# A conditioned residual stack on one core: both grouped convolutions moved to sixteen 32x32 tiles of TensorE, on unrounded fp32

## What is computed

```
# L0, L3: groups = 4 (32 channels in, 32 out each), 9 taps, padding 4
out = conv(x, weight, groups=4) + (c @ c_weight.T)[:, :, None] + bias[None, :, None]
# L1, L2: 8 experts, att = softmax(mlp(c)), one set of shares per sample
agg_w = einsum('bk,koi->boi', att, weight)
out   = einsum('boi,bih->boh', agg_w, x) + (att @ bias_k)[:, :, None]
# the chain
x = x + L0(x); x = x + L1(x); x = x + L2(x); x = x + L3(x)
```

## Time and profile before

| | |
|---|---|
| median of 3 executions | 2600.23 us |
| profiled execution | 2600.42 us |
| its span in the trace | 2598.5 us |
| TensorE busy | 2554.9 us, 98% of the span, 11082 matmul records |
| TensorE weight loads busy | 2071.6 us, 80% |
| VectorE busy | 2277.4 us, 88% |
| ScalarE busy | 2077.8 us, 80% |
| DMA | 808.75 MB moved, 311 GB/s on average |

### The profile page before, as it was taken

How to read it: one execution, slowest core, us unless ns; L and a number is a source line. 1 busy time by engine, 2 the same in 40 slices (tenths; PEclk the granted TensorE clock), 3 DMA queues, 4 the chain that set the end, 5 groups by cost and what they waited for, 6 DMA issues and landing times.

```text
span 2598.5 us, 38320 instructions
## 1 busy us (share of the span) xinstructions
PE 2554.9 (98%) x11082; PEld 2071.6 (80%) x11082; DVE 2277.4 (88%) x3384; ACT 2077.8 (80%) x1940; POOL 3.7 (0%) x17
## 2 busy tenths in 40 slices
PE   6999999999999999999999999999999999999997
PEld 4788888888888888888888888888888888888885
DVE  7988888888888888888888888888888888888884
ACT  4788878888887888888788888878888887888885
POOL 0000000000000000000000000000000000000000
PEclk8999999999999999999999999999999999999998
DMA  5788888888888888888888888888888888888875
GB/s 193 284 317 317 320 318 314 321 324 316 317 320 318 313 321 324 316 316 320 318 314 321 324 316 316 321 318 313 321 323 317 317 320 317 315 320 322 317 300 210
DMA packets 335448, 808.75 MB, mean 311 GB/s; under 512 B 37066, under 2 KB 40146, under 8 KB 302674
## 3 DMA queue, kind: packets, MB, share of 16 engines
q1 hardware_dynamic: 333200, 807.16, 83.5%
q10 hardware_dynamic: 2242, 1.53, 0.2%
HBM read 137.45 MB, written 134.22 MB: 105 GB/s over the span
## 4 chain that ended last, share of the span: by engine, by line
PE 97%; DVE 2%; issue 0%; DMA 0%; ACT 0%; ACTq 0%; SPq 0%; DVEq 0%
PE pair L766 82%; PE quad L810 14%; PE pair L800 1%; DVE mixed L595 0%; PE quad L747 0%; DMA x_in<-in_x 0%; DVE w_hi L528 0%; DVE weighted L583 0%; DVE x_lo L504 0%; DVE x_lo L630 0%; DVE x_hi L627 0%; DMA x_ph<-x_ch 0%; DVE x_ch L569 0%; DVE w_lo L534 0%; DMA x_ch<-x_ph 0%
## 5 line engine op out<-in xcount | busy, mean ns | idle before, releaser
L766 PE MATMUL pair<-x_hi,w_hi 128*128 128x512 f32 x3072 | 1227.1, 399 | 8.7 <-DVE x_lo L643 5.4
L766 PE MATMUL pair<-x_hi,w_lo 128*128 128x512 f32 x3072 | 1213.1, 395 | 0.0
L766 PE MATMUL pair<-x_lo,w_hi 128*128 128x512 f32 x3072 | 1209.0, 394 | 0.0
L766 PEld LDWEIGHTS pair<-x_hi,w_lo 128*128 128x128 f32 x3072 | 579.6, 189 | 137.3
L766 PEld LDWEIGHTS pair<-x_hi,w_hi 128*128 128x128 f32 x3072 | 579.0, 188 | 136.4 <-DVE x_lo L643 5.8
L766 PEld LDWEIGHTS pair<-x_lo,w_hi 128*128 128x128 f32 x3072 | 581.6, 189 | 131.5
L595 DVE TENSOR_REDUCE mixed<-weighted 128x128 f32<-128x1152 f32 x256 | 576.9, 2254 | 0.1
L402 ACT COPY x_out<-x_ch 128x1024 f32<-128x1024 f32 x256 | 530.3, 2073 | 2.9 <-DMA x_ch<-x_ph 2.9
L351 ACT COPY x_ch<-x_in 128x1024 f32<-128x1024 f32 x256 | 531.0, 2076 | 1.9 <-DMA x_in<-in_x 1.9
L410 ACT COPY x_ph<-pair 128x512 f32<-128x512 f32 x512 | 314.8, 615 | 272.1 <-PE pair L766 272.1
L418 ACT ACTIVATE x_ph<-pair,bias_now 128x512 f32<-128x512 f32 x512 | 358.6, 700 | 216.2 <-PE pair L766 216.2
(11 more groups left out here) (80 smaller groups left out, 607.2 us busy)
## 6 DMA issues: line engine op xcount, KB each, us to landing
x_ph<-x_ch SPq DMA_DIRECT2D x1024, 256.0 KB, 2.6
x_ch<-x_ph SPq DMA_DIRECT2D x1024, 256.0 KB, 2.6
x_in<-in_x SPq DMA_DIRECT2D x128, 1024.0 KB, 5.5
out<-x_out SPq DMA_DIRECT2D x128, 1024.0 KB, 4.2
x_out<-in_W SPq DMA_DIRECT2D x8, 144.0 KB, 5.4
expert<-in_e ACTq DMA_DIRECT2D x2, 512.0 KB, 8.0
x_ph<-in_e_t SPq DMA_DIRECT2D x1, 512.0 KB, 4.3
x_ph<-in_small ACTq DMA_DIRECT2D x1, 458.5 KB, 3.5
```

The source lines that it names most:

```text
L766: mm = nc.tensor.matmul(conv_bank[g % 2], w[l][:, m, g, :], x[:, g, m:m + N], start=(m == 0 and x is hi and w is w_hi), stop=(m == BLK - 1 ...
```

## The change

The convolutions no longer use phases, bands or rounded operands. x stays in channel rows as it is loaded. The array of TensorE is used as sixteen tiles of 32 x 32: the row tile is the group (its 32 input channels), the column tile is a quarter of the sequence (512 consecutive positions). A tap is a shifted window on the row, so a convolution is 9 taps x 4 quarters x 4 groups = 144 matmuls of 32 x 32 weights and 512 columns, in plain fp32. Their output has the rows (quarter, channel of the group) and one PSUM bank per group. The mixes read that layout: 4 groups x 3 products x 4 quarters = 48 `float32r` matmuls of 32 rows by 128 columns of weights, and write channel rows again, from which x3 is evacuated to SBUF as it is. x4 is stored to DRAM straight from the quarter layout, by four DMAs.

With this go: `cut`, `join`, `round_x`, `low_x`, `split_x3`, all four moves, the band and its splitting. New are: the split of x1 while it is evacuated (ScalarE rounds from PSUM, VectorE subtracts from PSUM), the sixteen `scalar_tensor_tensor` steps that sum the experts, and a way for the split matrix through DRAM (`save_m`, `spread_m`), which lays its rows in the order that the four row tiles need. One set of four PSUM banks serves even samples, the other odd ones. TensorE's loop takes two samples per turn.

```diff
-        conv_bank = bank[0:2]
-        mid_bank = quad
+        banks = [ctx.enter_context(nc.psum_tensor(f"banks{n}", [C, PH, N], f32)) for n in range(2)]
...
# SP
-            def step(b, slot, whole=True):
-                if whole or b >= 1:
-                    move_x3(b - 1)
-                move_x1(b, 0)
...
+            def save_m(b, slot):
+                sp.wait_ge(m_split, b + 1)
+                sp.dma_start(m_saved[slot, :, :, :], m_pair[:, :, :].bitcast(f32)).then_inc(m_stored, DMA)
+
+            def spread_m(b, slot):
+                sp.wait_ge(m_stored, DMA * (b + 1))
+                for q in range(PH):
+                    sp.dma_start(m_rows[rows_of(q), slot, :, :, :].bitcast(f32),
+                                 m_saved[slot, :, :, :].rearrange("(g c) t o -> c g t o", g=G)
+                                 ).then_inc(m_spread, DMA)
+
+            def store(b, slot):
+                sp.wait_ge(x4_ready, 2 * b + 2)
+                rows = out[b, :, :].rearrange("(g o) (p n) -> p o g n", g=G, p=PH)
+                for p in range(PH):
+                    sp.dma_start(rows[p], x4[rows_of(p), slot, :, :]).then_inc(x_stored[slot], DMA)
+
+            def step(b, slot, early=B, load_next=True, last=False):
+                if early >= 2:
+                    store(b - 2, slot)
+                if not last:
+                    save_m(b + 1, 1 - slot)
+                if load_next:
+                    load(b + 2, slot)
+                if not last:
+                    spread_m(b + 1, 1 - slot)
...
# ScalarE
+            def high_x1(b, tile):
+                act.wait_ge(conv1_done, b + 1)
+                for half in range(2):
+                    nc.scalar.copy(halves(x1_hi, half), halves(tile, half)).then_inc(x1_high, 1)
...
+            def step(b, slot, turn, early=B):
+                if early >= 1:
+                    evacuate_x3(b - 1, 1 - slot, banks[1 - slot])
+                high_x1(b, banks[slot])
+                if early >= 1:
+                    evacuate_x4(b - 1, 1 - slot, turn - 1 + slot, banks[1 - slot])
...
# VectorE
+            def mix_experts(b):
+                for k in range(K):
+                    for l in range(2):
...
+                        nc.vector.scalar_tensor_tensor(mixed[l][:, :], expert[l][:, k, :],
+                                                       mix[l][:, b, k:k + 1],
+                                                       ident[:, :] if k == 0 else mixed[l][:, :],
+                                                       ALU.mult, ALU.add).then_inc(mix_ready[l], 1)
...
+            def step(b, slot, turn, early=B, mix_next=True, last=False):
+                set_biases(b, slot)
+                if not last:
+                    split_m(b + 1, banks[1 - slot])
+                if mix_next:
+                    mix_experts(b + 2)
+                low_x1(b, banks[slot])
+                if early >= 1:
+                    evacuate_x4(b - 1, 1 - slot, turn - 1 + slot, banks[1 - slot])
...
# TensorE
+            def conv_taps(l, row, tile, which):
+                for t in which:
+                    for p in range(PH):
+                        for g in range(G):
+                            mm = nc.tensor.matmul(tile[rows_of(p), g, :], taps[l][rows_of(g), t, g, :],
+                                                  row[rows_of(g), N * p + t:N * p + t + N],
+                                                  start=(t == 0), stop=(t == TAPS - 1))
+                return mm
...
+            def middle(b, slot, tile):
+                pe.wait_ge(m_spread, DMA * G * (b + 1))
+                pe.wait_ge(x1_split, 2 * b + 2)
+                for g in range(G):
+                    for part, x in ((0, x1_hi), (0, x1_lo), (1, x1_hi)):
+                        for q in range(PH):
+                            mm = nc.tensor.matmul(tile[:, q, :], m_rows[rows_of(q), slot, g, part, :],
+                                                  x[rows_of(q), g, :],
+                                                  start=(g == 0 and part == 0 and x is x1_hi),
+                                                  stop=(g == G - 1 and part == 1))
+                mm.then_inc(mid_done, 1)
+
+            FIRST = range(0, 4)
+            REST = range(4, TAPS)
+
+            def step(b, slot, turn, last=False):
...
+                pe.wait_ge(x_loaded[slot], loaded)
+                wait(pe, x4_ready, evacuated)
+                conv_taps(0, x_in[:, slot, :], banks[slot], FIRST)
+                pe.wait_ge(x3_ready, 2 * b)
+                if not last:
+                    middle_matrix(b + 1, banks[1 - slot])
+                conv_taps(0, x_in[:, slot, :], banks[slot], REST).then_inc(conv1_done, 1)
+                pe.wait_ge(taps_ready, 2)
+                if not last:
+                    pe.wait_ge(m_ready, b + 2)
+                conv_taps(1, x3, banks[1 - slot], range(TAPS)).then_inc(conv4_done, 1)
+                middle(b, slot, banks[slot])
```

More of the change, by code:

```diff
@@ L229, in wait, with halves @@
                 eng.wait_ge(s, value)
+        def halves(tile, half):
+            return tile[:, half * PH // 2:(half + 1) * PH // 2, :]
         block = ctx.enter_context(nc.Block())
@@ L323, in _ @@
+            save_m(0, 0)
+            spread_m(0, 0)
+            for b in range(ODD):
+                step(b, b, early=b)
+            with sp.Fori(1, B // ODD - 1) as i:
+                for odd in range(ODD):
+                    step(ODD * i + odd, odd)
+            for b in range(B - ODD, B):
+                step(b, b % ODD, load_next=False, last=(b == B - 1))
+            for b in range(B - ODD, B):
+                store(b, b % ODD)
             for slot in range(ODD):
-                sp.wait_ge(x_stored[slot], DMA * B // ODD)
+                sp.wait_ge(x_stored[slot], DMA * PH * B // ODD)
@@ new lines, in evacuate_x4, with evacuate_x3 @@
+            def evacuate_x4(b, slot, turn, tile):
+                wait(act, x_stored[slot], DMA * PH * turn)
+                act.wait_ge(bias4_ready, b + 1)
+                act.wait_ge(conv4_done, b + 1)
+                for g in range(G // 2):
+                    done = nc.scalar.activation(x4[:, slot, g, :], tile[:, g, :], ACT.Identity,
+                                                bias=bias4_now[:, slot, g:g + 1])
+                done.then_inc(x4_ready, 1)
+            def evacuate_x3(b, slot, tile):
+                act.wait_ge(bias3_ready, b + 1)
+                act.wait_ge(mid_done, b + 1)
+                for half in range(2):
+                    columns = x3[:, EDGE:L + EDGE].rearrange("c (p n) -> c p n", p=PH)
+                    nc.scalar.activation(halves(columns, half), halves(tile, half), ACT.Identity,
+                                         bias=bias3_now[:, slot:slot + 1]).then_inc(x3_ready, 1)
@@ L690, in _ @@
[L690 to L704 removed]
+            dve.wait_ge(experts_loaded, 2 * DMA)
@@ new lines, in _ @@
+            dve.wait_ge(mix_copied, 4)
+            mix_experts(0)
+            low_x1(0, banks[0])
+            split_m(0, banks[1])
+            dve.wait_ge(bias_l_ready, 1)
+            carry_bias(0)
+            mix_experts(1)
+            carry_bias(1)
+            dve.wait_ge(vec_summed, 6)
+            dve.wait_ge(bias4_all, 1)
+            set_biases(0, 0)
+            split_m(1, banks[1])
+            mix_experts(2)
+            add_residual(1)
+            for b in range(1, 2 * ODD):
+                step(b, b % ODD, b // ODD, early=b)
@@ L707, in _ @@
+            with dve.Fori(2, B // ODD - 1) as i:
+                for odd in range(ODD):
+                    step(ODD * i + odd, odd, i)
+            for b in range(B - ODD, B):
+                step(b, b % ODD, b // ODD, mix_next=False, last=(b == B - 1))
+            evacuate_x4(B - 1, 1, B // ODD - 1, banks[1])
         @block.tensor
         def _(pe):
+            def conv_taps(l, row, tile, which):
[6 more added lines that the diff above has]
+                return mm
@@ L814, in step @@
[L814 to L818 removed]
             pe.wait_ge(bias4_all, 1)
+            pe.wait_ge(bias_l_ready, 1)
             pe.wait_ge(expert_t_loaded, DMA)
             expert_vectors(0)
[L825 to L827 removed]
+            pe.wait_ge(mix_copied, 4)
+            middle_matrix(0, banks[1])
+            middle(0, 0, banks[0])
```

668 lines of the change are left out of this document (180 added, 488 removed).

## The result

The changed kernel takes 3328.2 us (median of 4 runs, 3315.15 to 3333.55), the kernel before beside it 2599.93 (4 runs, 2599.28 to 2600.25): 1.279 times the time, 95% interval 1.276 to 1.283. The direction was forecast, the size (2795) was not.

A forecast was written before the change was run, and what follows sets the result against it. TensorE's own stream bounds the kernel, 19.79 us per sample. After the change 15.4 + 5.4 + 0.2 + 0.4 = 21.4 us; 60 + 127 x 21.4 + 16 = 2794, about 2795 us, range 2400 to 3750.

The forecast's parts named there:

- the forecast's own case: Whole kernel: slower, 2,610 to 3,300 us around the forecast of 2795, chance 0.40.
- rival 2: TensorE's issue: a load-matmul pair has a fixed shortest time; at 40 ns some 3,700 us; chance 0.12 beyond 3,300.
- Both signs named for a wrong prediction: TensorE per sample: a pair of the convolutions over 32 ns, or the mixes under 3.9 us.
- Columns, before and after: TensorE's matmuls: column streaming sets the cost, the change removes none; at best 19 ns per matmul, 1.6 us per sample.
- I take the data's 15.4 us: Convolutions: 576 weight loads work beside the data's 576 x 26.7 ns, so 15.4 us per sample.
- Rival 3: Convolutions: an fp32 matmul's halves queue on one tile, at most two tiles run; 129 us per sample, 16,400 us; chance 0.11.
- Mixes: 48 loads at 113 ns are 5.4 us: Mixes: 128-column weight loads follow one another on one port, 5.4 us per sample, ends 2.8 and 5.4.
- rival 1: TensorE: loads of different tiles go side by side, mixes 2.8 us; 18.8 us per sample, 2466 us; chance 0.33.
- Matrix and tile changes: TensorE per sample: matrix 0.23 us as before, four changes of tile shape 0.4 us, between 0 and 0.64.
- I count 0: Instruction fetch at TensorE's loop turns: 0 to 161 us, from 2.6 us in 62 turns; counted as 0.
- Covers: ScalarE, VectorE and DMA work stays hidden behind TensorE: counted as nothing; a cover failing by 0.5 us costs 64 us.
- The start: Before the first full step: the chain to the two first samples' matrices takes 60 us, between 50 and 75.

The follow-up runs named there:

- bf16 kernel: The changed kernel with both convolutions on the upper halves of the fp32 words, read as bf16, one pass instead of four: 2009.34 us.
- cols256: The changed kernel with taps 1 to 8 of both convolutions on 256 of their 512 columns: 3307.15 us.
- unrolled: The changed kernel with TensorE's loop written out, no jump back: 3128.51 us.

## Why the prediction was wrong in size

Two steps failed, both by setting a price at nothing: that of a second matmul on the same tile, and that of the fetch. A third, the mixes' loads, was too high and hid 300 us of it. The time lies inside the stated range of 2400 to 3750 by luck: it is above the forecast's own case, which ended at 3,300, and the range reached further only for rival 2's slow pairs. Both signs named for a wrong prediction came: a pair of the convolutions costs 19.35 us / 576 = 33.6 ns, over 32, and the mixes 3.0 us, under 3.9.

- **Columns, before and after: right.** The change takes no column time away; the records pass their columns four times, and a tap never goes under 853 ns.
- **"I take the data's 15.4 us" (the convolutions): the first step that failed.** Measured 19.35. The pair of load and matmul, on which the step turned, isn't the limit: inside a run pairs start some 16 ns apart, under the 27 forecast. What the step lacked is 222 ns per tap, 18 taps, 4.0 us per sample, some 507 us. Of these, 188 ns per tap, 430 us, are the price of two matmuls in succession on one tile; the rest lies at the ends of the stretches. Rival 3 had the mechanism (the halves queue up) and a size that was far off: the line is held up once in some 33 records, not at each tile.
- **"Mixes: 48 loads at 113 ns are 5.4 us": wrong, in the other direction.** Measured 3.0, four row tiles starting within 10 to 20 ns, every 230 to 235 ns: loads of different row tiles do go side by side. Here rival 1 was right. Some 300 us less. Matrix and tile changes cost 0.42 instead of 0.6, 25 us less.
- **"I count 0" for the fetch: the second step that failed.** It happens in each turn and costs 5.9 us, 62 x 5.9 = 366 us, over twice the upper end of 161, which took a data landing of 2.6 us as the nearest price. A turn of some 0.2 MB (12.48 MB in 62 turns) comes in about twelve transfers, two of them for the jump, in a stream that has hardly any slack, beside 2.8 MB of data per sample (354.11 / 128); that isn't one landing.
- Rival 2's figure of 3,700 for 40 ns pairs, which set the upper end of the range, doesn't follow from its own price: 2795 + 13 x 80 is 3,835. Nothing else rests on it.
- Together: 2795 + 507 - 300 - 25 + 366 = 3343, against 3328 measured.
- **Covers: right.** No wait for ScalarE or VectorE inside the loop; ScalarE 21%, VectorE 34%. A step of the experts is 345 ns where 280 were taken from the earlier trace rows, which changes nothing. The start (first full step at 55.0 instead of 60) was near. The cover was not thick: at two taps of conv4 it fails.
- The Trainium skill, "Runtime: NRT & Kernel Launch", section "Instruction fetch mechanics", was right in kind, and its effect should have been in the forecast rather than beside it: a taken branch whose target isn't in the current window of instructions waits for a DMA fetch. The traces agree that a loop body which is too long pays at each jump, 5.9 us here. Its 2048 instructions for TensorE are not what these runs show as the edge, which lies between 1,608 and 1,864 records (1,625 and 1,881 instructions in a turn of the traces). The 10.6 times that the Trainium skill gives in "TensorE: Matmul & The Clock Gate", Part 3, came out as 288 x 0.853 / 19.35 = 12.7 for plain fp32.

Could the idea be saved? Not at this precision. Unrolled and with most of the traffic gone it costs 22.8 us per sample against 19.79 before; with the traffic it has to carry, 24.1. The bf16 kernel takes 2009 us, below the kernel before, but by leaving the lower bits out. Splitting each fp32 into bf16 parts and taking three products, the second and third a round later, was not tried; as an estimate, 3 x 229 ns for a tap would be 12.4 us per sample, but some 1,830 records at 19 ns are 35 us, and 29 us at the 15.7 measured with little data, so the supply would forbid it.

## What to carry to other kernels

Count instructions as well as columns when a matmul is cut into small tiles: the stream has a supply of its own (here 16 ns per record with little data beside it, 17.5 to 19 beside all of the kernel's), a loop body that no longer fits pays 4 to 6 us per jump, and the transfers of instructions in the DMA queue's row (16 to 19, or over 570) tell which side a kernel is on. Don't let two matmuls on one small tile follow each other directly where it can be avoided; plain fp32 does it by itself. And a cut of work that leaves the total unchanged, as cols256, is the quickest sign of a second bound just below the first.

## What was unexpected of the hardware

- A second matmul directly behind the first on the same 32x32 tile holds up the line by some 190 ns once in 33 or 34 records. For the 32 records of a tap that is 629 against 458 ns in bf16, and 1041 against 853 of columns in fp32.
- Loads of 128 columns into different row tiles start mostly 1 to 9 ns apart, where pairs one by one had cost 113 ns.
- Instruction fetch suffers from the kernel's own data: the same stream costs 24.1 us per sample beside all of it and 22.8 with 93 MB of 354 left.
- Starving can cost twice. A gap of 3.73 us for want of instructions (cols256) was followed by a granted clock of 0.50 (1.2 GHz) from 1016 to 1021. In the changed kernel the gap of 2.86 us shown left it at 1.00, but it fell to 0.50 after the jump in 27 of 62 turns, for some 106 us in all. These samples are 0.4 us longer than the others (28.9 against 28.6, medians), while unrolled, without such gaps, kept 1.00 from its first full step to the last few us.
